# A third table of sums for the scatter-adds of an edge diffusion on a graph

## The reference

```python
h = jnp.maximum(_layernorm(x), 0.0)
h = h @ W.T + b
row = concat([src, loops]); col = concat([dst, loops])     # each node also has an edge to itself
deg = segment_sum(ones, row)
norm = deg**-0.5 [row] * deg**-0.5 [col]
agg = segment_sum(norm[:, None] * h[col], row)             # for each src: the sum over its edges
x = x + (h + 0.05 * (agg - h) + 1.5 * relu(h))
```

## Time and profile before

| what | value |
|---|---|
| time, median of 3 runs | 7401.49 us (7392.78 to 7404.23) |
| span of the profiled execution, first to last instruction | 7386.2 us |
| scatter-adds of the edge stage, POOL L893 | 392, 608.5 us busy, 410.9 us idle before them |
| loads and stores of the closing pass | 49 of 512 KB each from two tables, 49 stores |
| whole kernel, busy | PE 63%, DVE 61%, POOL 51%, ACT 22% |

### The profile page before, as it was taken

The page is one execution under the profiler, slowest core; times in us unless marked ns, Lnnn a source line. Parts: engine busy times, 40 slices in busy tenths (PEclk is TensorE's granted clock), DMA queues, the critical chain, the costliest instruction groups (busy, mean ns, idle before and its releaser), DMA issues. The chain is left out here.

```text
span 7386.2 us, 101314 instructions
## 1 busy us (share of the span) xinstructions
PE 4675.6 (63%) x31722; PEld 4192.0 (57%) x31722; DVE 4503.1 (61%) x5720; ACT 1623.3 (22%) x2242; POOL 3795.4 (51%) x3348
## 2 busy tenths in 40 slices
PE   4665335760188785555555866666668774784797
PEld 2354334650177785555555866666568774674675
DVE  6998443222577786666667842232398894683457
ACT  0143112330143343222222421111134340000001
POOL 0198565563277403777771047777600006766766
PEclk9866668995599998766767987777789996997899
DMA  2298666656722374332333753334357883122009
GB/s 75 48 276 259 140 147 140 138 108 201 252 73 73 101 245 154 83 79 79 81 78 101 249 164 109 109 109 112 100 186 250 304 307 112 49 59 91 14 12 278
DMA packets 837873, 1024.59 MB, mean 139 GB/s; under 512 B 589119, under 2 KB 601812, under 8 KB 836380
## 3 DMA queue, kind: packets, MB, share of 16 engines
q1 hardware_dynamic: 534716, 742.63, 31.5%
q0 software_dynamic: 144256, 90.12, 8.3%
q10 hardware_dynamic: 158560, 187.31, 7.6%
HBM read 608.19 MB, written 417.84 MB: 139 GB/s over the span
## 5 line engine op out<-in xcount | busy, mean ns | idle before, releaser
L839 POOL DMA_INDIRECT gc_msgs<-t,src_rows x784 | 754.4, 962 | 1098.1 <-POOLq L146 804.2
L893 POOL DMA_INDIRECT acc<-de_sums,de_put x392 | 608.5, 1552 | 410.9 <-DMA acc<-de_sums,de_put 263.5
L1913 PEld LDWEIGHTS gc_ring<-gc_msgs,gc_hot 128*128 128x128 f32 x4736 | 628.4, 210 | 305.9 <-issue 298.1
L1913 PE MATMUL gc_ring<-gc_msgs,gc_hot 128*128 x4736 | 654.9, 297 | 230.4 <-SPq L1872 229.3
L839 POOL DMA_INDIRECT at2s_ends<-h,src_rows x392 | 369.9, 944 | 533.6 <-POOLq L146 414.4
L839 POOL DMA_INDIRECT at1s_ends<-x,src_rows x392 | 389.2, 993 | 490.5 <-POOLq L146 371.3
L1027 PE MATMUL de_ring<-de_win,de_pick 128*128 x2368 | 343.2, 305 | 272.7 <-DMA de_win<-t 272.7
L1027 PEld LDWEIGHTS de_ring<-de_win,de_pick 128*128 128x128 f32 x2368 | 322.9, 217 | 295.0 <-issue 289.1
L839 POOL DMA_INDIRECT at1s_ends<-x,dst_rows x392 | 419.0, 1069 | 119.5 <-issue 119.5
L839 POOL DMA_INDIRECT re_rows<-x,src_rows x392 | 406.5, 1037 | 125.1 <-issue 124.8
L1393 PE MATMUL re_psR<-w_rel,re_own 128*128 128x128 f32 x3136 | 398.6, 293 | 73.6 <-DVE re_own L1330 73.3
(11 more groups left out here) (471 smaller groups left out, 11359.4 us busy)
## 6 DMA issues: line engine op xcount, KB each, us to landing
rew_win<-x SPq DMA_DIRECT2D x74, 544.0 KB, 4.0
at1w_win<-g SPq DMA_DIRECT2D x74, 544.0 KB, 4.0
at2w_win<-g SPq DMA_DIRECT2D x74, 544.0 KB, 4.0
de_near<-same SPq DMA_DIRECT2D x74, 512.0 KB, 5.1
de_win<-t SPq DMA_DIRECT2D x74, 512.0 KB, 4.6
x<-rew_win SPq DMA_DIRECT2D x74, 512.0 KB, 2.9
h<-at1w_win SPq DMA_DIRECT2D x74, 512.0 KB, 2.9
h<-at2w_win SPq DMA_DIRECT2D x74, 512.0 KB, 2.9
```

The source lines that it names most:

```text
L839: nc.gpsimd.indirect_dma_start(buf[:, t * width:(t + 1) * width], None, table, bass.IndirectOffsetOnAxis(ap=rows[:, t:t + 1], axis=0)).the ...
L893: nc.gpsimd.indirect_dma_start(g.acc0[j % 2], bass.IndirectOffsetOnAxis(ap=put[:, j:j + 1], axis=0), sums[:, j * D:(j + 1) * D], None, com ...
L1913: done = nc.tensor.matmul(ring[:, bass.ds(to[n], SLOT)], hot[k][:, n, :], each_group(msgs[:, bass.ds(of[n], MID)], SLOT // MID), start=Fal ...
```

## The change

A third table `acc0[2]` is added. Tile j goes to table j % 3 and waits for tile j-3. The new table has to start at zero, so SP stores 49 chunks of zeros into it while out degrees are counted, and waits there until they have landed. Setup clears the spare rows of one more table. The closing pass loads a third tile in each chunk and adds it.

```diff
+SUMS = 3
-        g.acc0 = [node_table(f"acc0{k}", D) for k in range(2)]
+        g.acc0 = [node_table(f"acc0{k}", D) for k in range(SUMS)]
...
     with Room(nc, g, "deg") as r:
+        zeroed = r.sem("zeroed")
         with nc.Block() as block:
+            @block.sync
+            def _(sp):
+                for c in range(STEPS):
+                    sp.dma_start(chunk_of(g.acc0[SUMS - 1], c), g.zeros[:, :]).then_inc(zeroed, 16)
+                sp.wait_ge(zeroed, 16 * STEPS)
...
-                        if j >= 2:
-                            held(pool, added[j % 2], 16 * (j // 2), g.passed)
-                        nc.gpsimd.indirect_dma_start(g.acc0[j % 2], bass.IndirectOffsetOnAxis(ap=put[:, j:j + 1], axis=0),
-                                                     sums[:, j * D:(j + 1) * D], None, compute_op=ALU.add).then_inc(added[j % 2], 16)
+                        if j >= SUMS:
+                            held(pool, added[j % SUMS], 16 * (j // SUMS), g.passed)
+                        nc.gpsimd.indirect_dma_start(g.acc0[j % SUMS], bass.IndirectOffsetOnAxis(ap=put[:, j:j + 1], axis=0),
+                                                     sums[:, j * D:(j + 1) * D], None, compute_op=ALU.add).then_inc(added[j % SUMS], 16)
...
                     sp.dma_start(base[b.slot][:, :], chunk_of(g.acc0[1], b.number)).then_inc(x_in[b.slot], 16)
                     sp.dma_start(acc[b.slot][:, :], chunk_of(g.acc0[0], b.number)).then_inc(x_in[b.slot], 16)
+                    sp.dma_start(more[b.slot][:, :], chunk_of(g.acc0[2], b.number)).then_inc(x_in[b.slot], 16)
...
-                    dve.wait_ge(x_in[s], 32 * b.nth)
+                    dve.wait_ge(x_in[s], 48 * b.nth)
                     link(nc.vector.tensor_tensor(base[s][:, :], base[s][:, :], acc[s][:, :], ALU.add))
+                    link(nc.vector.tensor_tensor(base[s][:, :], base[s][:, :], more[s][:, :], ALU.add))
```

## The result

The changed kernel takes 7344.28 us, median of 4 runs (7342.41 to 7347.64), where the kernel before takes 7402.86 us in 4 runs (7392.78 to 7418.66): a ratio of 0.9914 with a 95% interval of 0.9897 to 0.9930, 58.6 us less. The forecast was 7380 us with a range from 7362 to 7402 us; the direction was right, the gain almost three times as large.

The account below looks back on a forecast made before the run. It took POOL's waits for scatter-add landings, and the tail they leave after the blocks, as the edge stage's bound. -89 us there and +67.5 us in the closing pass gave -21.5 us: 7401.5 to 7380 us, range 7362 to 7402.

Parts of the forecast that it names:

- By the blocks: Edge stage: ACT's last block copy and the last batch of 8 tiles put POOL's last scatter-add start at 1645.6 us.
- the floor of 1.85 us: Edge stage: least time per scatter-add on POOL, 1.55 us for the instruction and 0.30 us for the gap behind it.
- The upper bound by landings: Edge stage: POOL's 215 remaining starts at the floor plus 58 us for landings over 4.75 us: last start at 1654 us.
- Rival 1: Edge stage: three scatter-adds in flight land no faster than two, nothing gained, kernel 7469 us; chance 0.11, fully or in part.
- the price of the closing pass: Closing pass: 49 more loads cost 65 us, and with the ends 67.5 us, on top of 220.5 us.
- At the present 94.7% of use: Closing pass: the added loads' 61 us divided by 0.947, the present use, gives 65 us.
- lower price of 61 us: Closing pass: 49 more loads at 421 GB/s, 1.25 us for each 512 KB, as the low end of their cost.
- -89 us: Edge stage: POOL's last scatter-add start moves from 1738.8 us to 1650 us, the gain from three tables.
- The 60.5 us drawn from the first: Closing pass: cost of the added 25.7 MB at the skill's 425 GB/s, for a total change of about -26 us.
- priced at nothing: Degree stage and setup: 63 us of clearing stores hide beside DVE's counting, and one more setup store fits SP's slack.
- Rival 2: Edge stage: denser scatter-adds slow PE's row loads before 1215 us, blocks finish 14 us later, kernel 7392 us; chance 0.12.
- Rival 3: Closing pass: added loads pay in full, 73 us and the ends, 75.5 us, kernel 7388 us; chance 0.11.

Follow-up runs that it names:

- e1: The kernel before with 6 slots instead of 4 in the closing pass alone: 7370.20 us, ratio 0.9965 to the kernel before; the pass takes 190.2 us.
- e2: The kernel before with a third load per closing-pass chunk, waited for but not added, and no third table: 7433.34 us, ratio 1.0047 to before.
- e6: The changed kernel with a fourth table, cleared, added into and loaded in the closing pass: 7405.77 us, ratio 1.0010 to the kernel before.
- e7: The changed kernel with 6 slots instead of 4 in the closing pass: 7331.32 us, ratio 0.9908 to the kernel before; the pass takes 254.6 us.
- e9: The kernel before with 3 slots instead of 4 in the closing pass: 7441.04 us in one run; the pass takes 249.3 us.
- e4: The changed kernel without its third closing-pass load, the third table's sums left out of the output: 7299.85 us, ratio 0.9867 to the kernel before.

## Why the prediction was wrong

**The edge stage was right.** "By the blocks" gave 1645.6 us for the last start, the sum used 1650, and 1646.2 came. The landing waits fell as described, the floor of 1.85 us and the 0.99 us from copy to start held, and POOL waited for blocks before about 1200 us (72.4 of the 76.3 us) and near the end. The upper bound by landings, 1654 us, was too careful: between 1215 and 1632 us POOL waited 55.6 us for landings in 50 gaps. Of these some 15 us are the 0.30 us that any gap has, so landings cost some 41 us above the floor, less than the estimate's 58, and POOL caught up with the blocks before they ended. Rival 1, landings that come later with three under way, did not come about: 4.2 us instead of 4.3.

**The step that failed is the price of the closing pass**, "+67.5 us", and in it the sentence that puts the added loads "At the present 94.7% of use". That took the DMA share for how full the engines were, and so left no idle time in the pass that the added bytes could fill. The pass moved 350 GB/s; with 6 slots the same transfers ran at 405 GB/s over the pass, with the same tables (e1), so 30 us of its 220.5 were waiting for slots. A third load in each round brought the added bytes and took up those 30 us: 33.1 us without the third table (e2), 34.8 with it. On engines that are full the same load costs 63 us (e6 over the change) or 64 us (e7 over e1, 254.6 - 190.2), close to the forecast's lower price of 61 us and to the 65 us that it took. The term was mis-sized by 33 us, which is most of the 37 us between the forecast change of -21.5 us and the measured -58.6. The rest lies in the edge stage: -89 us was forecast, and it gave -93 against the profile of before, -99 against the mean of the five profiles with two tables; the interval of the measured change does not tell these apart.

The rows for the right reading were there. In the earlier trace rows the rate swings between 232 and 422 GB/s while the DMA share of the earlier trace rows is 0.95. I noted it, and put it down to loads beside stores; but in e1 loads and stores stand in the same proportion and no slice in the middle falls under 417. Nor did I set the time of a chunk against what its transfers need. At the 1.28 us that a store of 512 KB takes of all engines, three transfers need some 3.8 us, but a chunk took 220.5 / 49 = 4.5 us.

The Trainium skill ("DMA: Bandwidth & Descriptors", section Bandwidth) has 425 GB/s for a transfer of 16 MB on a core whose neighbour is idle and about 358 GB/s as HBM's limit for a core. These runs, on one core, come near the first: 413 to 425 GB/s in the middle slices of every pass that was not short of slots. That the mean of before, 350 GB/s, lay near the second is an accident of its 4 slots: the same transfers ran at 310 GB/s with 3 (e9) and at 405 with 6 (e1). The 60.5 us drawn from the first is an estimate for full engines, which the pass before did not have.

**What was priced at nothing cost nothing.** The clear's stores were issued from 102.2 to 161.7 us, and the degree stage kept its 210 us, also with two clears in e6. Setup's end did not move: DVE's first one-hot of the degree stage starts at 105.3 us, before at 106.2.

**Rival 2, later blocks**, shows in a small way. From POOL's first scatter-add to the end of ACT's last copy the five profiles with two tables have 872 to 878 us, the three with three tables 879 to 880, the one with four 882. That is some 5 us for the third table where the forecast took 2. **Rival 3**, a closing pass that pays 75.5 us, was the opposite of what came.

Two things are not shown. What holds up the long packets stays open: 7% of the load packets take over 250 ns in the passes that are short of slots (before, e4, e9) and under 1% in those that are not (the change, e1). And the part behind the closing pass differs by up to 15 us between executions of any of these kernels, for which no cause was looked for; nor was one for the 12 us by which the edge stage with two tables differs.

## What to carry to other kernels

A DMA share near 1 does not say that the engines are full; compare the rate with the best that the same kind of transfer reaches in any slice, and the time of a chunk with what its transfers take of the engines. Where a loop has few slots, first work out a slot's round: as long as the round sets the pace and leaves the DMA engines gaps, an added transfer costs less than its length (here 33 to 35 us of 63), and once the gaps are filled it costs its full length, so that the second price can't be read from the first. A gain that is read from one profile of before carries that profile's luck: five with two tables ended the same stage up to 12 us apart. And what a chain of waits can give back ends where the work that feeds it ends: here three tables gave all there was in the edge stage, and the fourth gave nothing more and cost 63 us in the closing pass.

## What the runs showed of the hardware

Scatter-adds into three tables, 201 of them in 417 us while the DMA engines moved 138 GB/s in all, land no later than 155 into two tables did beside 134 GB/s (median 4.2 us from issue, 4.3 before). With four tables, 200 of them beside 139 GB/s, the median is 3.9 us (e6): a third and a fourth scatter-add under way did not delay the landings. Loads and stores mixed two to one ran at 417 to 422 GB/s on one core (e1), three loads to one store at 415 to 421 (the change), four to one at 413 to 420 (e6), all in the middle slices of the pass. A larger share of stores did not make a fed pass slower.
